# Replacing two thirds of the indirect scatters of node sums by single-row transfers from SyncE, in a two-layer graph network kernel

## The reference

```python
# layer 0: for every edge e = (src, dst), a 16 x 16 message and a 16 x 16 attention logit
w_m = (efeat @ W_msg + b_msg).reshape(E, 16, 16);  w_a = (efeat @ W_attn + b_attn).reshape(E, 16, 16)
e1, e2 = w_m * x[src][:, :, None], w_a * x[src][:, :, None]
ex = jnp.exp(e2 - segment_max(e2, dst)[dst])
ft = segment_sum(e1 * ex / segment_sum(ex, dst)[dst], dst).sum(axis=1)
x = _layernorm(x + ft)
# layer 1: the mean of the edge features at each node
x = _layernorm(x + segment_sum(edge_attr, dst) / max(count, 1))
```

## Time and profile before

| | us |
|---|---|
| time, median of three runs | 3261.99 |
| span of the profiled execution, first to last instruction | 2263.2 |
| median less span | 998.8 |
| GpSimd busy | 1705.7 (75%) |
| TensorE busy | 1987.7 (88%) |
| VectorE busy | 1868.1 (83%) |
| last node-sum scatter issued | 1923.3 |

### The profile page before, as it was taken

How to read it: one execution, slowest core, us unless ns; L and a number is a source line. 1 busy time by engine, 2 the same in 40 slices (tenths; PEclk the granted TensorE clock), 3 DMA queues, 4 the chain that set the end, 5 groups by cost and what they waited for, 6 DMA issues and landing times. The chain is left out here.

```text
span 2263.2 us, 21991 instructions
## 1 busy us (share of the span) xinstructions
PE 1987.7 (88%) x6770; PEld 904.0 (40%) x6770; DVE 1868.1 (83%) x2907; ACT 1294.5 (57%) x1240; POOL 1705.7 (75%) x1863
## 2 busy tenths in 40 slices
PE   2658989998999998899998898899998989899996
PEld 0313434443444443444444343344444434344442
DVE  6757778887888878888987897797878878899985
ACT  5335556655666656565664665555655556556653
POOL 6777777777777777777777777777777777777776
PEclk9769999999999999999999999999999999999998
DMA  7111111111111111111111111111111111111100
GB/s 283 33 13 13 13 16 13 13 13 13 13 13 13 13 18 13 12 13 15 15 12 12 17 12 12 17 12 12 16 12 16 12 15 12 36 11 22 14 7 4
DMA packets 60441, 47.69 MB, mean 21 GB/s; under 512 B 28654, under 2 KB 55919, under 8 KB 59804
## 3 DMA queue, kind: packets, MB, share of 16 engines
q0 software_dynamic: 58000, 29.82, 10.6%
q1 hardware_dynamic: 2316, 16.38, 1.9%
HBM read 44.09 MB, written 1.90 MB: 20 GB/s over the span
## 5 line engine op out<-in xcount | busy, mean ns | idle before, releaser
L634 POOL DMA_INDIRECT AR<-in_xt,AR x1628 | 1559.8, 958 | 498.6 <-issue 487.0
L1104 PE MATMUL PX<-AR,CS 128*128 128x512 f32 x3290 | 1574.3, 603 | 5.7 <-ACT AR L870 5.5
L1408 DVE CUSTOM_DVE_ANT_1 AR<-PW,AR 128x1024 f32<-128x1024 f32 x826 | 987.2, 1220 | 173.7 <-PE PW L1084 116.9
L1104 PEld LDWEIGHTS PX<-AR,CS 128*128 128x128 f32 x3290 | 628.8, 192 | 580.2 <-issue 457.9
L1084 PE MATMUL PW<-WS,LT 100*128 100x512 bf16 x1652 | 512.0, 395 | 189.9 <-DVE AR L1408 188.8
L1421 DVE TENSOR_TENSOR AR<-AR,PX 128x1024 f32<-128x1024 f32 (+1 forms) x448 | 507.9, 1134 | 81.9 <-ACT PX L920 54.7
L864 ACT ACTIVATE LT<-PTB 100x1024 bf16<-100x1024 bf16 (+1 forms) x224 | 214.1, 956 | 514.8 <-PE PTB L1073 514.8
L922 ACT ACTIVATE AR<-AR 128x2048 f32<-128x2048 f32 (+1 forms) x224 | 435.7, 1945 | 7.3
L926 ACT ACTIVATE PX<-AR 128x1024 f32<-128x1024 f32 (+1 forms) x224 | 219.1, 978 | 297.1 <-DVE AR L1421 294.1
L1084 PEld LDWEIGHTS PW<-WS,LT 100*128 100x128 bf16 x1652 | 144.1, 99 | 569.5 <-issue 292.2
L920 ACT ACTIVATE PX<-AR 128x1024 f32<-128x1024 f32 (+1 forms) x224 | 236.7, 1057 | 21.2 <-DVE AR L1421 19.7
(11 more groups left out here) (168 smaller groups left out, 499.8 us busy)
## 6 DMA issues: line engine op xcount, KB each, us to landing
AR<-in_xt,AR POOLq DMA_INDIRECT x1628, 2.4
AR<-in_eat SPq DMA_DIRECT2D x3, 3128.0 KB, 16.6
AR<-in_eat SPq DMA_DIRECT2D x1, 3120.0 KB, 12.2
AR<-in_es,AR POOLq DMA_INDIRECT x49, 3.4
y_d<-AR SPq DMA_DIRECT2D x1, 784.0 KB, 7.4
AR<-y_d SPq DMA_DIRECT2D x1, 784.0 KB, 4.6
y_d<-AR POOLq DMA_INDIRECT x36, 2.1
CS<-in_cst SPq DMA_DIRECT2D x1, 442.0 KB, 5.3
```

The source lines that it names most:

```text
L634: g.indirect_dma_start(feat(h, j - j0, j - j0 + 1), None, xt, bass.IndirectOffsetOnAxis(ap=XE[:, at:at + 1], axis=0)).then_inc(hg_sem(h), 16)
L1104: i = pe.matmul(PDR, IDN, x, start=(a == 0 and j == 0), stop=(g == LAST[k] and j == n - 1))
L1408: v.tensor_tensor_reduce(em(g, j, j + 2).rearrange("p (x c) -> p x c", c=32), w, hb, 1.0, LOW, ALU.mult, ALU.max, accum_out=MXC[:, k % 2, ...
```

## The change

The 36 tiles are split: BY_TILE = 2, 5, 8, ..., 35 (12 tiles) keep GpSimd's indirect scatter. BY_ROW (24 tiles) are written by SyncE. VectorE casts NODE to float, TensorE transposes it, and VectorE multiplies it by 128 and casts to int32: ROWS[k, p] is the byte offset in YD of the row of node p of tile k, with tile k on partition k. For each tile by row, SyncE waits for a_out and v_sa, then four times loads 32 offsets into 32 registers (one TENSOR_LOAD) and issues 32 DMAs of one row of 128 bytes each, each behind a register move (`snap`). The wait ahead of the load of YD now covers the four semaphores of the row transfers and the 12 scatters.

```diff
+BY_ROW = [k for k in range(MAIN) if k % 3 != 2]
+BY_TILE = [k for k in range(MAIN) if k not in BY_ROW]
@@ registers, names and semaphores
+        NODF, ROWS = RID[:, 0:NC], RID[0:NC, 64:192].bitcast(i32)
+        d_yr = d_st
+        S.update(v_nf=S["v_pc"], p_nf=S["p_o"], v_rows=S["v_gi"])
@@ SyncE, regular()
-                sp.wait_ge(S["d_y"], 16 * MAIN)
+                to = [sp.alloc_register(f"row_{i}") for i in range(32)]
+                flat = YD.bitcast(mybir.dt.uint8).rearrange("n w -> (n w)")
+
+                def rows(x, k):
+                    sp.wait_ge(S["a_out"], k + 1)
+                    sp.wait_ge(S["v_sa"], k + 1)
+                    for q in range(4):
+                        sp.reg_load(to, ROWS[k:k + 1, 32 * q:32 * q + 32])
+                        for i in range(32):
+                            at = sp.snap(to[i])
+                            p = 32 * q + i
+                            sp.dma_start(flat[bass.ds(at, 128)].unsqueeze(0), OUTR[p:p + 1, k, :].bitcast(mybir.dt.uint8))\
+                              .then_inc(d_yr[x % 4], 16)
+
+                sp.wait_ge(S["v_rows"], 1)
+                for x, k in enumerate(BY_ROW):
+                    rows(x, k)
+                for b in range(4):
+                    sp.wait_ge(d_yr[b], 16 * 128 * len(BY_ROW[b::4]))
+                sp.wait_ge(S["d_y"], 16 * len(BY_TILE))
@@ GpSimd, regular()
-                    if 5 <= k < MAIN + 5:
+                    if k - 5 in BY_TILE:
                         results(k - 5)
@@ TensorE, gsum() and regular()
+                            if g == 0:
+                                pe.wait_ge(S["v_rows"], 1)
+                    if i == 3:
+                        pe.wait_ge(S["v_nf"], 1)
+                        pe.transpose(PX[0:NC, 2, 0:128], NODF[:, :], IDN).then_inc(S["p_nf"], 1)
@@ VectorE, regular()
+                    if i == 2:
+                        v.tensor_copy(NODF, NODE).then_inc(S["v_nf"], 1)
+                    if i == 4:
+                        v.wait_ge(S["p_nf"], 1)
+                        v.tensor_scalar(ROWS[:, :], PX[0:NC, 2, 0:128], 128.0, None, ALU.mult).then_inc(S["v_rows"], 1)
```

## The result

The changed kernel takes 3834.7 us (median of four runs, 3817.4 to 3846.5), the kernel before 3267.7: a ratio of 1.17 (95% interval 1.167 to 1.176), 567 us slower. The forecast was 3231, and its range ended at 3640. On another chip the changed kernel took 3853.8 us beside 3305.9 before, a ratio of 1.164 (1.156 to 1.173); 3800 to 3850 had been expected of it there.

What follows compares the result with a forecast made beforehand. The prediction took GpSimd's issue of indirect DMAs as the bound: 31.0 us saved there, offsets and SyncE's rows costing 0, so 3261.99 - 31.0 = 3231.0 us, with a range of 3222 to 3640.

Steps and rivals of the forecast that it cites:

- What bounds the kernel: GpSimd's unbroken issue of indirect DMAs sets the pace from about tile 20; VectorE waits 63.6 us for gathers.
- what lies around the span: The 998.8 us between profiled span (2263.2) and median time, kept unchanged in the forecast.
- GpSimd's part: On GpSimd, 24 scatters of 1.29 us each go; 31.0 us saved, followed in full by VectorE.
- The offsets: Small VectorE instructions, a transpose and TensorE waits at the start: under 1 us, hidden by GpSimd's lead, counted 0.
- SyncE's part: SyncE's 3072 row transfers make YD ready at 265.4 + 3072 c, before VectorE needs it; break-even 0.539 us, cost nothing.
- c: SyncE's period for one row transfer with its share of everything: 0.497 us, with ends 0.362 and 1.241.
- (1): SyncE's DMA instruction for one row: 0.345 us, bounds 0.262 and 0.627; a register address can only add.
- (2, 3): On SyncE, per row: the pause to the next instruction, 0.046 us, and one register move with its pause, 0.09.
- (4): SyncE's load of 32 registers costs what one register does: 0.016 us a row; 0.473 if each costs its own trip.
- Rival 2: SyncE's register loads cost by the register, making YD late; 4505 us at the full 0.473 each; chance 0.12.
- Rival 1: SyncE's row transfer itself is too slow, from a 0.387 us DMA on, making YD late; 3357 to 3888 us; chance 0.22.
- Rival 3: The compute engines don't follow GpSimd's saving, which becomes TensorE's waits; about 3262 us, or some 3250; chance 0.07.

Runs made afterwards that it cites:

- Experiment 1: Kernel before, unchanged: 3272.8 us, profiled span 3273.2; changed kernel with all 36 scatters kept on GpSimd, offsets still made: 3274.6 us (0.999).
- experiment 2: Changed kernel with 12 tiles by row instead of 24: 3360.8 us (1.027 of before); with 24 at static addresses, no register loads or moves: 3353.3 (1.025).
- experiment 4: Kernel before without the 36 main-tile scatters and nothing in their place: 3308.6 us (1.009); on another chip 3335.6 (1.010).

## Why the prediction was wrong

**What bounds the kernel.** Wrong for the timed chips. "GpSimd is never idle for more than 0.3 us" is true of the profile shown, but not of the executions that were timed, where VectorE, ScalarE and TensorE wait for late completions and GpSimd waits for VectorE. The warning stood in the front table: a median 998.8 us above the span. The step by which what lies around the span "is kept as it is: the profile has nothing on it" took a contradiction for a constant. Nearly 1000 us that the profile can't place say that the profile is of another execution, and its bound needn't be the timed one's. Experiment 1 showed that there is nothing around the span.

**GpSimd's part, -31.0 us.** Not had. On the 3270 kind, 36 scatters fewer gave +29 us, not -46. On the 2265 kind half the gathers, over 1000 us of GpSimd's issue, gave 79, so there was little more to be had there.

**The offsets, 0.** Right: 0.999.

**SyncE's part, c = 0.497.** Wrong, and decisive. Term by term, as measured undisturbed: (1) the DMA instruction 0.227 us, against 0.345 taken; that is under the low bound of 0.262. That a register address "can only add" was wrong too: with a static address the median was 0.252. (2, 3) Two moves and the pauses, 0.387 - 0.227 = 0.16, against 0.136 for one move and a pause. (4) The register load 6.78 / 32 = 0.21, against 0.016. The sum is 0.60, with small pauses 0.615 to 0.62, past the prediction's break-even of 0.539; with 0.016 in place of 0.21 it would have been about 0.41.

**The two steps that failed.** The first is term (4), the short end taken "because all 32 words lie side by side on one partition and one instruction asks for them". The Trainium skill ("Runtime: NRT & Kernel Launch", section "Instruction fetch mechanics") has about 200 ns for each register, for loads from HBM. For these loads from SBUF the trace agrees: 212 ns. On the 2265 kind, from whose profile the sum was made, this step alone explains the outcome: with 0.615 the prediction's own formula gives YD at 265.4 + 3072 x 0.615 = 2155 us, and the change with half the gathers had its load of YD issued at 2159.0.

On the timed chips that step alone would have cost nothing. There SyncE starts at 417 us and VectorE would look at YD at 2922.6, so the break-even is (2922.6 - 417 - 7) / 3072 = 0.81 us a row, and rows at 0.615 would be out at 2306, some 600 us early. The second step that failed is that c holds each instruction's price alone and no term for the other engines' work beside it. The runs showed 0.46 us a row more while they run (1.08 against 0.62), and 0.97 over all. Static rows without loads and moves took 0.44 beside the same work, so the surcharge needs the loads and moves too, or grows with them. Where it comes from stays open. It is gone in the stop and on the 2265 kind. In after's trace, up to 2900 us, the intervals between two row DMAs that last over 1 us (loads left out) hold 0.66 indirect DMAs of GpSimd per us, the shorter ones 0.31. But GpSimd stands in the stop like all the others, and spacing the gathers brought the 34.6 us for 32 rows only to 31.4.

**Rival 2** named the mechanism of the first step, with about half its price, and deserved more than 0.12. The estimate by the page's figure, some 3670 us, was nearer than the forecast, but partly by luck: it has the right load price on a break-even of the other kind of chip and without the surcharge. **Rival 1** was wrong in its mechanism: the row DMA's median is 0.227 us, not over 0.387. What it would have looked like, a row that takes longer than its instruction's price, did come, from the second step. **Rival 3** was right in its result (the saving isn't followed), for another reason than the one named.

**The sum, as it came out** in the two profiled executions: lateness 480 us, 70 us that were lost before it, 8 fewer behind it, nothing saved on GpSimd: 542. The medians have 567. The cause of the 480 is shown. Of the 70, experiment 2 shows that they come with rows that are never late, and experiment 4 leaves open how much of them is a matter of GpSimd's changed order.

**The range** reached to c = 0.673 and would have held the undisturbed row price of 0.615; it left out what the other engines' work beside SyncE adds, and the 1000 us by which the profile differed from the timed runs.

## What to carry to other kernels

When the span and the time disagree by hundreds of microseconds, stop: the profile may be of another condition than the timed runs, and its bound is then no basis for a sum. Price a many-register load by the register, and count a transfer with a register address as its DMA plus every register instruction in front of it. Don't take these prices, read on an idle core, for the pace beside busy engines. A long unbroken series of indirect DMAs on GpSimd can hold the other engines up though none of them waits for it: look whether their stands end with the series, and try to space it.

## What was not expected of the hardware

- Chips, or conditions of them, differ by 1000 us on the same program: 2264.6 us on one, 3271 to 3306 on five. VectorE's, ScalarE's and GpSimd's busy times are alike to within 1%; the difference shows as TensorE's completions, 2.9 us late in the mean on the slower kind and 0.0 on the other. Its granted clock is 0.96 of full on the faster kind and 0.83 on the slower. TensorE's own busy time differs by 171 us (1988 and 2159), so the clock can't be the whole of the 1000; since TensorE stands more where it is lower, the clock may follow from the stands rather than cause them.
- On the 3270 kind, fewer gathers give back over a microsecond each: 802 of them 883 us, 1.10 us each, where their issue takes 1.25 us of an engine that isn't the bound. Half of that (440 us) comes back also if they are all kept and a fill of 0.30 us is put behind each.
- A load of 32 registers from SBUF takes 6.7 to 6.9 us in the median, on both kinds of chip.
- A one-row DMA takes SyncE 0.227 us to issue with a register address and 0.252 us with a static one (medians); the single row, L495, took 0.428. Its whole period, with two moves, is 0.387, with its share of the load 0.62, and beside the running engines of the 3270 kind 1.08.
- 3072 DMAs of one row that are never late cost some 83 us in all, and 24 DMAs of the same bytes 18; up to some 29 us of each may come from the missing scatters.
- On the 3270 kind the profile lacks up to a quarter and more of VectorE's semaphore updates (1489 of 2064 are there), on the 2265 kind none.
